# Block-wise attention inside an LSTM recurrence: y copied by ScalarE and multiplied by GpSimd, zero matmuls ahead of waiting work

## What is computed

```python
m  = einsum('bsi,io->bso', x * ys[:, None, :], weight) * d[:, None, :]   # modulation by cond
qkv = m @ ternary(w_qkv).T                       # 16 heads of 8, 4 key/value heads
q, k = rotary(rms_norm(q)), rotary(rms_norm(k))
y  = softmax(causal(q @ k.T * scale)) @ v        # per head
x1 = x + rms_norm(y) @ ternary(w_proj).T         # y normalised over the 128 features
a  = x1[t] @ Wx + b + h @ Wh                     # LSTM over the 128 positions
i, f, o, g = sigmoid, sigmoid, sigmoid, tanh of the quarters of a
c  = f * c + i * g ; h = o * tanh(c)
out = x1 + gated_ffn(h)                          # fake-quantised weights and activations
```

## Time and profile before

| | us |
|---|---|
| median of 3 runs | 327.45 |
| lowest, highest | 327.13, 332.43 |
| the profiled execution | 328.31 |
| its span | 326.5 |
| busy in it: PE, DVE, ACT, POOL | 259.7, 227.0, 181.3, 70.4 |

### The profile page before, as it was taken

One profiled execution on the slowest core, in us unless ns is written; L12 is line 12 of the kernel. 1 busy time (PEld: TensorE's weight loads), 2 busy tenths in 40 slices (PEclk: granted clock), 3 DMA queues, 4 the chain that ended last, 5 costly groups with the idle time before them and its releaser, 6 DMA issues.

```text
span 326.5 us, 8995 instructions
## 1 busy us (share of the span) xinstructions
PE 259.7 (80%) x3354; PEld 158.9 (49%) x3354; DVE 227.0 (70%) x1075; ACT 181.3 (56%) x566; POOL 70.4 (22%) x95
## 2 busy tenths in 40 slices
PE   2628957998989999998898989889888888757233
PEld 1427735656675556565555656554444444322100
DVE  5887885788876767776866875555565655567775
ACT  4338984765757767577526665643244242259480
POOL 3712155920001049400100000010000000006533
PEclk9955975999967999999879997997999999987855
DMA  4324301000001000000000000000000000000003
GB/s 92 103 55 111 68 0 32 3 2 2 5 3 32 2 3 2 3 4 1 2 2 3 3 2 2 1 2 2 0 3 3 0 3 2 0 0 3 0 0 128
DMA packets 7355, 5.59 MB, mean 17 GB/s; under 512 B 1680, under 2 KB 6032, under 8 KB 7312
## 3 DMA queue, kind: packets, MB, share of 16 engines
q1 hardware_dynamic: 7024, 4.89, 6.1%
...
## 4 chain that ended last, share of the span: by engine, by line
PE 45%; DVE 27%; ACT 18%; issue 6%; DMA 1%; SPq 0%; ACTq 0%; DVEq 0%; POOL 0%
PE bank L1332 16%; PE bank L1391 8%; ACT tanh_c L990 5%; ACT gates_sb L985 4%; DVE h_hi L1837 4%; DVE prod L1829 4%; DVE gates_sb L1832 4%; PE bank L1251 3%; PE bank L1054 3%; DVE neg_max L1616 3%; PE bank L1192 2%; PE bank L1242 2%; PE bank L1136 2%; DVE h_ffn L1904 1%; PE bank L1099 1%
## 5 line engine op out<-in xcount | busy, mean ns | idle before, releaser
L1391 PE MATMUL bank<-ident_b,zero_w 128*128 128x512 bf16 x272 | 78.6, 389 | 0.0
L985 ACT ACTIVATE gates_sb<-bank 128x64 f32<-128x64 f32 x128 | 28.7, 224 | 65.6 <-PE bank L1332 62.2
L1332 PEld LDWEIGHTS bank<-h_hi,wh_hi 128*128 128x128 f16 x508 | 23.8, 98 | 70.6 <-DVE h_hi L1837 63.7
L1829 DVE SCALAR_TENSOR_TENSOR prod<-gates_sb 128x32 f32<-128x32 f32 x128 | 24.6, 192 | 38.8 <-ACT gates_sb L985 34.9
L1332 PE MATMUL bank<-h_hi,wh_hi 128*128 128x16 f16 x508 | 33.0, 173 | 22.3 <-DVE h_hi L1837 21.5
L990 ACT ACTIVATE tanh_c<-gates_sb 128x16 f32<-128x16 f32 x128 | 27.7, 216 | 41.3 <-DVE gates_sb L1832 38.2
L1837 DVE TENSOR_TENSOR h_hi<-o_scaled,tanh_c 128x16 f16<-128x16 f32 x128 | 22.5, 176 | 25.7 <-ACT tanh_c L990 25.4
L1332 PE MATMUL bank<-h_lo,wh_hi 128*128 128x16 f16 x508 | 32.6, 172 | 0.0
L1391 PEld LDWEIGHTS bank<-ident_b,zero_w 128*128 128x128 bf16 x272 | 22.5, 99 | 20.6 <-issue 9.8
L1251 PE MATMUL bank<-x1T,wx_sb 128*128 128x128 f32 x128 | 31.3, 335 | 0.0
L1332 PE MATMUL bank<-h_hi,wh_lo 128*128 128x16 f16 x508 | 31.1, 170 | 0.0
...
## 6 DMA issues: line engine op xcount, KB each, us to landing
...
```

Of the source, the lines that this page charges most:

```text
L985: A.activation(gates_sb[:, now, 0:GATES * B], bank[(t // BANK_STEPS) % 2][:, slot:slot + GATES * B], ACT.Tanh, scale=scale).then_inc(gates ...
L1332: ins = E.matmul(bank[dst][:, col:col + B], w[:, g * P:(g + 1) * P], h[:, part, :], start=False, stop=True, skip_group_check=True)
L1391: E.matmul(bank[1 - ((t + 1) // BANK_STEPS) % 2][:, :], zero_w[:, :], ident_b[:, :].unsqueeze(1).broadcast_to([P, 4, P]), start=False, sto ...
L1829: V.scalar_tensor_tensor(out=prod[:, :], in0=G[:, now, 0:2 * B], scalar=1.0, in1=G[:, now, 3 * B:5 * B], op0=ALU.add, op1=ALU.mult).then_i ...
```

## The change

y of blocks 1 to 3, once turned into a PSUM bank, is copied by ACT to y_turn in SBUF (turned_tile_out); DVE takes the reciprocal from there (invert), and POOL multiplies (normalise, now of all blocks). All copies of block 1's yT and lowered queries are on ACT. Of the zero matmuls of a step with lowered queries or score columns, up to two go ahead of that work. The tables shift accordingly, and FILLER is new. head_norms(3) starts its first half on the first half of the sums. The diff, cut to its core:

```diff
-        QK_POOL = {(2, 0): 3, (2, 1): 3, (3, 0): 6, (3, 1): 8}
+        QK_POOL = {(2, 0): 3, (2, 1): 3, (3, 0): 6, (3, 1): 9}
...
-        QT_OUT_AT = {2: ((20, 21), (24, 25), (30, 31), (36, 37)), 3: ((52, 53), (56, 57), (62, 63), (68, 69))}
+        QT_OUT_AT = {2: (None, None, (30, 31), (36, 37)), 3: ((52, 53), None, (62, 63), (68, 69))}
+        QT_OUT_B = {(2, 0): 21, (2, 1): 24, (3, 1): 56}
...
-        ROWS_AT = {1: ((2, 3), (5, 7)), 2: ((21, 23), (27, 29), (33, 35), (39, 41)),
+        ROWS_AT = {1: ((2, 3), (5, 7)), 2: ((22, 23), (27, 29), (33, 35), (39, 41)),
...
-        MQ_OUT_AT = {1: (8, 9, None, None), 2: (28, 34, 40, 46), 3: (60, 66, 72, 78)}
-        MQ_OUT_DVE = {1: (None, None, 12, 13)}
+        MQ_OUT_AT = {1: (8, 9, 12, 13), 2: (28, 34, 40, 46), 3: (60, 66, 72, 78)}
...
-        PV_AT = {1: ((15, 15), (17, 17)), 2: ((33, 34), (39, 40), (45, 46), (51, 52)), 3: ((65, 66), (71, 72), (77, 78), (83, 84))}
-        YT_AT = {1: (None, None, 18, None), 2: (35, 41, 47, 53), 3: (67, 73, 79, 85)}
-        YT_DVE_AT = {1: (16, 17, None, 19), 2: (None,) * 4, 3: (None,) * 4}
-        TURN_AT = {1: (17, 18, 19, 20), 2: (36, 42, 49, 53), 3: (68, 74, 81, 85)}
-        NORM_AT = {1: (19, 20, 21, 22), 2: (38, 44, 50, 54), 3: (70, 76, 82, 86)}
-        Y_SQUARE_AT = {1: (20, 21, 22, 23), 2: (39, 45, 51, 55), 3: (71, 77, 83, 87)}
-        Y_SCALE_AT = {1: 24, 2: 56, 3: 88}
-        YN_AT = {1: 24, 2: 56, 3: 88}
-        YN_OUT_AT = {1: 25, 2: 57, 3: 89}
-        PROJ_AT = {1: 25, 2: 57, 3: 89}
-        X1_AT = {1: (26, 27), 2: (58, 59), 3: (90, 91)}
+        PV_AT = {1: ((14, 14), (17, 17)), 2: ((33, 34), (39, 40), (45, 46), (51, 52)), 3: ((65, 66), (71, 72), (77, 78), (83, 84))}
+        YT_AT = {1: (16, 17, 19, 20), 2: (35, 41, 47, 53), 3: (67, 73, 79, 85)}
+        TURN_AT = {1: (16, 18, 19, 20), 2: (36, 42, 49, 53), 3: (68, 74, 81, 85)}
+        TOUT_A = {1: (18, None, None, None), 2: (38, 44, 51, None), 3: (70, 76, 83, None)}
+        TOUT_B = {1: (None, 19, 20, 21), 2: (None, None, None, 54), 3: (None, None, None, 86)}
+        Y_SQUARE_AT = {1: (20, 21, 22, 23), 2: (40, 46, 54, 56), 3: (72, 78, 86, 88)}
+        Y_SCALE_AT = {1: 24, 2: 57, 3: 89}
+        YN_AT = {1: 24, 2: 57, 3: 89}
+        YN_OUT_AT = {1: 25, 2: 58, 3: 90}
+        PROJ_AT = {1: 25, 2: 58, 3: 90}
+        X1_AT = {1: (27, 32), 2: (59, 64), 3: (91, 92)}
...
-        SUM_AT = (32, 33)
-        TRIG_A = {2: tuple(range(1, 9)), 3: (25, 26, 27, 28, 29, 32, 33, 34, 35, 38)}
-        TRIG_B = {2: (0, 4, 5, 6), 3: (26, 27, 29)}
-        ADD_AT = {2: (11, 11), 3: (39, 45)}
-        MUL_AT = {2: (14, 15), 3: (46, 47)}
-        HI_AT = {2: (15, 16), 3: (47, 48)}
-        DUP_AT = {2: (17, 18), 3: (49, 50)}
-        LO_AT = {2: (17, 18), 3: (48, 49)}
+        SUM_AT = (33, 38)
+        TRIG_A = {2: tuple(range(1, 9)), 3: (26, 27, 28, 29, 32, 33, 34, 35, 39, 41)}
+        TRIG_B = {2: (0, 4, 5, 6), 3: (27, 28, 29)}
+        ADD_AT = {2: (11, 12), 3: (44, 45)}
+        MUL_AT = {2: (13, 14), 3: (46, 47)}
+        HI_AT = {2: (14, 15), 3: (47, 48)}
+        DUP_AT = {2: (18, 18), 3: (49, 50)}
+        LO_AT = {2: (15, 16), 3: (48, 49)}
...
+        ZEROS_AHEAD = {t for k in (1, 2, 3) for t in MQ_AT[k]} | {t for k in (1, 2, 3) for u in COLS_AT[k] for t in u}
+
         FILLER = (
-            1, 2, 3, 2, 4, 2, 3, 1, 2, 3, 3, 1, 1, 2, 2, 0, 4, 0, 0, 0, 0, 0, 0, 2, 0, 0, 2, 3, 2, 1, 3, 4,
-            2, 2, 1, 2, 0, 1, 1, 2, 3, 2, 0, 3, 1, 1, 2, 3, 3, 0, 2, 2, 1, 0, 1, 3, 0, 0, 2, 3, 2, 1, 3, 3,
-            2, 1, 1, 2, 0, 1, 1, 1, 2, 2, 0, 3, 1, 1, 1, 3, 3, 0, 4, 1, 1, 0, 2, 4, 0, 0, 4, 3, 3, 3, 3, 4,
-            4, 4, 4, 3, 3, 3, 3, 4, 4, 4, 4, 3, 3, 3, 3, 4, 4, 2, 4, 3, 3, 3, 3, 4, 4, 4, 4, 4, 4, 4, 4,
+            1, 2, 3, 2, 4, 2, 3, 1, 2, 3, 3, 1, 1, 2, 0, 3, 2, 0, 0, 1, 1, 0, 0, 2, 2, 0, 2, 3, 2, 1, 3, 4,
+            2, 2, 1, 2, 1, 2, 1, 2, 3, 2, 2, 3, 1, 1, 2, 3, 3, 2, 2, 2, 1, 1, 2, 3, 4, 2, 0, 1, 2, 1, 3, 3,
+            2, 2, 1, 1, 1, 2, 1, 2, 2, 2, 2, 2, 1, 1, 1, 3, 3, 2, 4, 1, 1, 1, 3, 4, 4, 2, 0, 3, 3, 3, 3, 4,
+            4, 4, 4, 3, 3, 3, 3, 4, 4, 4, 4, 3, 3, 3, 3, 4, 4, 3, 3, 3, 3, 3, 3, 4, 4, 4, 4, 4, 4, 4, 4,
         )
...
+            def normalise(k, T):
+
+                n = TILES * k + T
+                gp.wait_ge(inverted, n + 1)
...
+                    G.tensor_tensor(out, y[:, :, 0:HD], w.unsqueeze(2).broadcast_to([P, HEADS, HD]), ALU.mult).then_inc(y_ready, 1)
...
             max_parts(1, 1)
+            for T in range(TILES):
+                normalise(1, T)
             row_norms(1)
...
             max_parts(2, 2)
+            normalise(2, 0)
             head_norms(3, slice(TILES // 2, TILES))
+            normalise(2, 1)
             max_parts(2, 3)
+            normalise(2, 2)
+            normalise(2, 3)
             row_norms(2)
...
+            max_parts(3, 1)
+            normalise(3, 0)
+            max_parts(3, 2)
+            normalise(3, 1)
+            max_parts(3, 3)
+            normalise(3, 2)
+            normalise(3, 3)
             row_norms(3)
...
+            def turned_tile_out(k, T):
+
+                n = TILES * (k - 1) + T
+                ac.wait_ge(turned, n + 1)
+                ac.wait_ge(y_ready, n + 1)
+                A.activation(y_turn[:, T, :].rearrange("p (h e) -> p h e", h=HEADS)[:, :, 0:HD + 1],
+                             bank[TURN_BANKS[k][T]][:, :].rearrange("p (h e) -> p h e", h=HEADS)[:, :, 0:HD + 1],
+                             ACT.Copy).then_inc(turned_out, 1)
...
+                for T in range(TILES):
+                    if T >= 2 and t == MQ_OUT_AT[1][T]:
+                        lowered_out(1, T)
+                    if t == YT_AT[1][T]:
+                        yT_out(1, T)
...
+                for h in range(2):
+                    if t == DUP_AT[2][h]:
+                        upper(2, h, 1)
...
-                emptied[TURN_BANKS[k][T]] = [(y_ready, TILES * k + T + 1)]
+                emptied[TURN_BANKS[k][T]] = [(turned_out, q + 1)]
...
             def side(t):
+                ahead = min(FILLER[t], 2) if t in ZEROS_AHEAD else 0
+                zeros(t, ahead)
...
+                zeros(t, FILLER[t] - ahead)
...
+            def invert(k, T):
+                n = TILES * (k - 1) + T
+                v.wait_ge(turned_out, n + 1)
+                V.reciprocal(recip[:, T, :], y_turn[:, T, :].rearrange("p (h e) -> p h e", h=HEADS)[:, :, HD]).then_inc(inverted, 1)
```

More of the change, by code:

```diff
@@ L634, in _ @@
             for T in range(TILES):
-                normalise_0(T)
+                normalise(0, T)
             row_norms(0)
@@ L641, in _ @@
             max_parts(1, 1)
+            for T in range(TILES):
+                normalise(1, T)
             row_norms(1)
-            for u in range(2):
-                max_parts(2, u)
+            max_parts(2, 0)
+            max_parts(2, 1)
             head_norms(3, slice(0, TILES // 2))
             max_parts(2, 2)
+            normalise(2, 0)
             head_norms(3, slice(TILES // 2, TILES))
+            normalise(2, 1)
             max_parts(2, 3)
+            normalise(2, 2)
+            normalise(2, 3)
             row_norms(2)
-            for u in range(UNITS[3]):
-                max_parts(3, u)
+            max_parts(3, 0)
+            max_parts(3, 1)
[5 more added lines that the diff above has]
+            normalise(3, 3)
             row_norms(3)
@@ L912, in side_a @@
                             upper(k, h, 0)
-                        if t == DUP_AT[k][h]:
+                        if k == 3 and t == DUP_AT[k][h]:
                             upper(k, h, 1)
@@ L930, in side_b @@
                     for T in range(TILES):
-                        if t == YT_AT[k][T]:
+                        if t == TOUT_B[k][T]:
+                            turned_tile_out(k, T)
+                        if k > 1 and t == YT_AT[k][T]:
                             yT_out(k, T)
@@ L949, in side_b @@
                         queries_out(1, T, 2)
+                for (k, T), at in QT_OUT_B.items():
+                    if t == at:
+                        queries_out(k, T, 2)
                 for h in range(2):
@@ L1347, in recur, with zeros @@
                         fill_piece(1 - dst, chunk, slot - (BANK_STEPS - GATES))
+            def zeros(t, n):
+                for _ in range(n):
+                    E.matmul(bank[1 - ((t + 1) // BANK_STEPS) % 2][:, :], zero_w[:, :],
+                             ident_b[:, :].unsqueeze(1).broadcast_to([P, 4, P]), start=False, stop=False, skip_group_check=True)
             def side(t):
+                ahead = min(FILLER[t], 2) if t in ZEROS_AHEAD else 0
+                zeros(t, ahead)
                 for k in range(1, BLOCKS):
@@ L1389, in side @@
                                     weigh_pairs(u)
-                for _ in range(FILLER[t]):
-                    E.matmul(bank[1 - ((t + 1) // BANK_STEPS) % 2][:, :], zero_w[:, :],
```

(10 more changed lines are left out.)

62 lines of the change are left out of this document (24 added, 38 removed).

## The result

The changed kernel takes 326.04 us in the median of 20 runs (324.25 to 328.37); the kernel before, beside it, 327.49 us (20 runs, 326.11 to 332.43). The ratio is 0.9959 with a 95% interval of 0.9939 to 0.9979: a small gain, 1.45 us, about half of the 2.85 that I had forecast. Medians and ranges here are of all executions; the ratios leave out those over 1.5% above the fastest of the same kernel.

The account below looks back on a forecast made before the run. No engine alone bounds it: a recurrence ring over PE, DVE and ACT, 1.76 us a step, with 11.2 us of side work above it. Terms sum to -2.8 us, 328.31 to 325.5; less 0.86 to the median, 324.6; range 321.3 to 328.7.

Parts of the forecast that it names:

- Part 3: New zero table keeps TensorE's clock up in most of five low-clock stretches: about 4.3 us saved, ends 0 and 5.3.
- Part 1: DVE gives away normalise and three yT copies, lower(2) earlier; steps 18, 20, 55: 0.73 us saved.
- Part 2: Zeros ahead of waiting work fall into an existing wait; steps 11, 32, 44, 64, 76: 1.65 us saved.
- Part 4: Lowered-query copies (1,2), (1,3) on ScalarE wait for PE ahead of tanh_c in steps 12, 13: 1.54 us lost.
- Part 5: weigh_pairs(0), moved from PE's step 15 to 14, runs past when the next recurrence is due: 0.6 us lost.
- Part 6: GpSimd's normalises ahead of max_parts delay the lowered queries three times, 0.27 us each: 0.8 us lost.
- Part 8: Added zeros in nearly full steps 53, 65, 71, 24 and ahead of lowered queries at 8, 9: 0.6 us lost.
- Part 7: Twelve GpSimd normalises beside DVE slow it by 0.03 us each: 0.36 us lost, ends 0 and 4.9.
- (a): Clock isn't held, falls may only move and none of the 4.3 us is won: 328.9 us; chance 0.17.
- (b): Clock falls once more in block 1, slowing steps 14 to 17, 1.5 us in all: 326.1 us; chance 0.16.
- (c): No stall from the ScalarE copies or weigh_pairs, as PE reaches this work sooner: 322.5 us; chance 0.15.
- (d): Each of 12 GpSimd normalises holds up DVE's ring by 0.41 us: 329.1 us; chance 0.04.

Follow-up runs that it names:

- e7: Changed kernel with the copies of lowered queries (1,2) and (1,3) behind tanh_c and the zero table of before: 338.12 us, ratio 1.0304.
- e17: Kernel before with three zero matmuls ahead of its first recurrent matmuls: 326.88 us, ratio 1.0002.
- e4: Changed kernel with its zero matmuls all behind the waiting work again, table left as it is: 328.54 us, ratio 1.0025.
- e2: Changed kernel with the zero table of before: 334.45 us, ratio 1.0174.
- e1: Changed kernel with the copies of lowered queries (1,2) and (1,3) moved behind tanh_c: 322.8 us, ratio 0.9863.
- e0: Changed kernel run again beside the kernel before, no edit: 326.35 us, ratio 0.9959.
- e16: Changed kernel with three zero matmuls ahead of the first recurrent matmuls and nothing else: 326.77 us, ratio 0.9989.
- e12: Changed kernel with copies (1,2), (1,3) behind tanh_c, queries' copy (2,1) in step 25, three zero matmuls ahead of the first recurrent matmuls: 321.59 us, ratio 0.9845.
- e6: Changed kernel with copies (1,2), (1,3) behind tanh_c, queries' copy (2,1) in step 25, weigh_pairs(0) in step 15, zeros shifted: 323.19 us, ratio 0.9891.
- e5: Changed kernel with GpSimd's max parts of (2,3), (3,2), (3,3) ahead of normalises (2,1), (3,0), (3,1): 324.71 us in one execution.
- e8: Changed kernel with two more zero matmuls behind the lowered queries' matmuls in each of steps 12 and 13: 326.27 us, ratio 0.994.

## Why the prediction was half right

What the traces of the two kernels hold above 1.76 us a step, us:

| trace (us) | steps 0-10 | from 11 on |
|---|---|---|
| before: 328.31, 327.06, 327.36, 328.94 | 1.05, 0.59, 1.10, 1.79 | 10.17, 9.66, 8.81, 10.37 |
| changed: 324.25, 324.94, 324.8, 326.14, 326.44 | 1.11, 1.90, 1.82, 2.93, 2.94 | 5.78, 6.38, 6.45, 5.82, 5.97 |

From step 11 on, where nearly all of the change lies, the means are 9.75 and 6.08: 3.7 us saved, more than the 2.8 of my sum. In steps 0 to 10, which it hardly touches, the changed kernel's traces lie 1.0 us higher. That leaves 2.7 us between these traces. The medians differ by less, 1.45, and among the executions that no trace shows are the changed kernel's slowest: six of 32, at clocks of 0.894 to 0.898, take 326.8 to 328.4 us.

**The step that failed** is the last one of the sum: "That execution lies 0.86 above the median of the timed runs, 327.45, so against the median I forecast **324.6 us**". It takes a saving worked out on one execution for the saving between the medians, and so it puts a difference in clock between one execution and another at nothing, without a reason. What the runs show in its place is a sum of three numbers. The two profiled executions differ by 4.06 us, 1.3 more than forecast. The one of before lies 0.82 above its median of 327.49. The changed kernel's lies 1.79 below its median of 326.04: 4.06 - 0.82 - 1.79 = 1.45. The 1.79 is matched by what the clock takes ahead of step 6: 15 of the changed kernel's 32 executions have a clock of 0.911 to 0.914 and take 325.1 to 326.6 us, and the two of this kind that were traced have 2.93 and 2.94 us of excess in steps 0 to 10, where the profiled one has 1.11. My sum has no term there. None of five traces of the kernel before has more than 1.8 there, but one of the old table under the new placement (e7) has 3.0; whether the change makes this early loss more frequent, or chance does, stays open.

Part 3 priced the clock from the earlier trace rows alone. Of those five stretches only the one around step 58 is in all five traces of the kernel before (e17's with them); and of its 115 executions beside the changed kernels five took under 325 us, as little as the changed kernel's best.

The other terms, by the first pair of traces and the runs:
- Part 1, DVE's relief, -0.73: steps 18, 20 and 55 at 1.77, 1.96 and 1.76, 5.49 against 6.44: -0.95. Step 20 as worked out, 55 better.
- Part 2, zeros ahead, -1.65: -1.48 in the steps, 1.26 of it shown by e4 to be the zeros' place.
- Part 3, -4.3: none of the low stretches of the first trace is left, -5.03. 23 keeps 0.21 at full clock, where I had 0.35. e2 shows that without the new table the rest of the change is a loss, 1.0174.
- Part 4, +1.54: step 12 was forecast to a few hundredths, tanh_c 1.46 us after gates (measured 1.48), and e1 wins 1.36 back in the steps. What the stalls cost beyond their own length was not in the sum: e1 against e0 2.2 us, e16 against e12 3.5 us of the medians.
- Part 5, +0.6: step 15 took 2.21, +0.45. e6 shows the alternative dearer.
- Part 6, +0.8: 0.15. The normalise delays the lowered queries as I said (they end at T+1.40 to T+1.47, in e5 at T+0.83 to T+0.95), but the last of them starts at T+1.18 to T+1.25, next to the recurrence's T+1.17, and only 0.03 to 0.07 a step comes through.
- Part 8, +0.6, the zeros' own price: against the kernel before steps 36, 38 and 81 are longer by 0.20, 0.14 and 0.24, and each stall holds 0.2 of it; right in size, though 53, 65 and 71 were named. Step 100 has 0.23 more than before in every variant: DVE's hidden starts 0.32 us after h_hi there, in the kernel before 0.09, and PE's h_lo matmuls come late by it. Why it starts late was not looked into.
- Part 7, +0.36: nothing. DVE's h_hi keeps 174/175/177 ns (shortest/median/longest) over all 128:

```profile
L1868 DVE TENSOR_TENSOR h_hi<-o_scaled,tanh_c x128: 174/175/177, 54.2 to 284.6; 128x16 f16<-128x16 f32 x128
```

That alone doesn't settle it, since no h_hi runs beside a normalise: these start at T+1.65 to T+1.85. What runs beside them is mostly prod, as at the end of step 19:

```profile
91.63 0.41 POOL L591 TENSOR_TENSOR y_tok<-y_turn,recip 128x128 f32<-128x128 f32 x1 [1.35 <-DVE recip L1686]
...
92.00 0.19 DVE L1860 SCALAR_TENSOR_TENSOR prod<-gates_sb 128x32 f32<-128x32 f32 x1 [0.45 <-ACT gates_sb L1030]
```

The eight prods that overlap a normalise took 173 to 193 ns, those with GpSimd idle 178 to 194. Beside other GpSimd work the ring was held a little: the cell's sum (L1863) took 232 to 248 ns in place of 174 four times, where it ran into the start of a power or a max_parts.
- x1 "is written in 59 and 91, just in time, so I count nothing": for blocks 2 and 3 that held (step 60 at 1.76), but block 1's residual, moved from 26 to 27 and needed in 28, I had not looked at: 0.3. And step 24, 0.4, where I had looked at side_a's gap only.

**The rivals.** (a), the clock isn't held, 328.9: in no trace of the changed kernel from step 11 on is more low than steps 25 and 26, 0.5 us together; the six executions at 0.894 to 0.898 were not traced. (b), 326.1: its time is nearly the measured one, but its mechanism is not shown, so that the match is luck as far as is known. Steps 14 to 18 are at full clock with 0.6 us of excess in every trace with stalls and the new table. That the stalls cost clock somewhere is supported by e0 against e1 and by e16 against e12, both by distributions of runs; zeros laid into the stalls (e8) did not mend the median, and where the clock falls in those executions stays open. (c), no stall: out, step 12. (d), GpSimd holds DVE for the 0.41 us of each normalise: out, by the prods above. The Trainium skill's rule of mutual exclusion for a whole instruction (SBUF — State Buffer, "Who interferes with whom") is not borne out here: 15 h_hi lie beside a power of 13.1 or 6.7 us, which reads SBUF, and none of the 128 was longer than 177 ns.
